# Three of eight one-hots of a group made by ScalarE, as relu(1 - (lane - place)^2), in the sums by source of a four-layer graph network

## Chip, cores and metric

The kernel runs on one core of a Trainium2 chip. The metric is the device time of one execution in microseconds (us); lower is better. The engines are TensorE (PE, with its weight loads as PEld), VectorE (DVE), ScalarE (ACT), GpSimd (POOL) and SyncE (SP).

## What is computed

Four graph layers run one after the other on 12,500 nodes with 64 features and 400,000 edges. Each starts with a layer norm and adds its result to x. The change touches the last one, whose core is

```python
i, j = edge_index            # i = src, j = dst
msg = x[j] + (edge_attr @ We + be)
agg = segment_sum(msg, i, num_segments=N)
h = (1.0 + eps) * x + agg
out = relu(h @ W1 + b1) @ W2 + b2
return (out - mu) * rsqrt(var + 1e-5) * gamma + beta
```

The segment sum goes by source, while the edges of the input lie in the order of their destination. What is summed for an edge is one row of 81 values: 64 features of the destination's x, a one, and 16 edge attributes.

## The kernel before

The kernel is a row of stages with a barrier between them. It sorts edges into slots and writes records, runs three layers that gather rows by indirect DMAs, and then, in `scatter_messages`, writes each edge's row to the DRAM array `rec2`. A row there has three bf16 parts of 81 values, which together carry the precision of f32, and one more value, the place (0 to 127) of the edge's source within its block of 128 nodes. That is 244 bf16 values, `ROW`. Padding rows have place -1. Four tiles of 128 rows (a quad) belong to one block.

The stage of the change, `source_sums`, reads `rec2` in 440 groups of 1,024 rows. A group is eight tiles (G = 8) and so two quads. All buffers form rings of eight groups (`RING2`); PSUM has a ring of four (`RING`). A loop has 55 turns and eight groups in each turn are written out (`q` = 0 to 7); the first turn is peeled. For each group

- SP issues the load of `rows[q]` (L1246), after the matmuls that read the buffer eight groups ago (`s_mm[q]`);
- ACT copies the eight places out of the rows to f32, `place[q]` (L1290), when the load has landed;
- DVE makes eight one-hots of 128x128 bf16 in `hot[q]` (L1272), by comparing the lane numbers `iotab` with a column of `place[q]`;
- PE multiplies each one-hot with the three parts of its tile, 24 matmuls of 81 columns (L1304), which leave one block sum of 128x81 for each quad;
- DVE adds the two block sums of the group before the last (`q - 2`) to `acc2` (L1265), at addresses that are read from `blks` into registers. The 16 registers of a whole turn are loaded together, in `add_group` for q = 0, so after the one-hots of q = 2.

The order on each engine is that of the code. DVE's is the one-hots of q, then the adds of q - 2. After this stage comes `last_stage`, which starts at a barrier.

Of the kernel before, what the change touches and what calls it, by code (L numbers as in the profile page):

```python
# [14 lines left out]
BF16 = mybir.dt.bfloat16  # L15
I32 = mybir.dt.int32
ALU = mybir.AluOpType
ACT = mybir.ActivationFunctionType
AX = mybir.AxisListType

P = 128
# [7 lines left out]
G = 8  # L29
# [5 lines left out]

QT = 4
RING2 = 8
QUADS = -(-((E + NB * (QT * P - 1)) // (QT * P)) // (G // QT * RING2)) * (G // QT * RING2)
GROUPS2 = QUADS * QT // G
SLOTS2 = QUADS * QT * P  # L40
EPS = 1e-5
# [12 lines left out]
ROW = PARTS * MW + 1  # L54
# [30 lines left out]
def wait_earlier(engine, semaphore, value):  # L85

    if not isinstance(value, int) or value > 0:
        engine.wait_ge(semaphore, value)
# [30 lines left out]
def build(nc, a, out):  # L119
    ctx = ExitStack()  # L120
    with ctx:
        sem = Semaphores(nc)
        rec = nc.dram_tensor("rec", (SLOTS + SPARE * G * P, RW), F32).ap()
        rec2 = nc.dram_tensor("rec2", (SLOTS2, ROW), BF16).ap()
        table = nc.dram_tensor("table", (NPAD, R * D), F32).ap()
        ptable = nc.dram_tensor("ptable", (NPAD, D), F32).ap()

        arena = ctx.enter_context(nc.sbuf_tensor("arena", [P, ARENA], F32))
        consts = Buffers(arena)
        iotaf = consts.take(P)  # L130
        ident = consts.take(P)
        iotab = consts.take(P // 2, BF16)
        identb = consts.take(P // 2, BF16)
        ones = consts.take(P)
        pidx = consts.take(1)
        epsc = consts.take(1)
        blkd = consts.take(TILES, I32)
        blks = consts.take(QUADS, I32)
        base = consts.at
        psum = ctx.enter_context(nc.psum_tensor("psum", [P, 4096], F32))  # L140

        b = Buffers(arena, base)
        ints, flts, srcl = b.take(2 * COLS, I32), b.take(2 * COLS), b.take(COLS)
        keys, off, padq = b.take(COLS, BF16), b.take(WIDE), b.take(QT * ROW // 2, BF16)
        lasts = b.take(2 * NB, I32)
        starts_stage(nc, sem, a, Buffers(arena, b.at), psum, iotaf, ident, iotab, identb, ones, pidx, epsc, blkd, blks,
                     ints, flts, srcl, keys, off, padq, lasts, rec, rec2)
        sem.end_stage()
        x = arena[:, ARENA - NB * D:ARENA]
        record_stage(nc, sem, a, b, psum, iotaf, ident, identb, epsc, ints, flts, srcl, keys, off, padq, lasts, x, rec, rec2, table)  # L150
        sem.end_stage()

        b = Buffers(arena, base)
        acc, h = b.take(NB * D), b.take(NB * D)
        shared = b.take(NB * PARTS * D // 2)
        hparts, acc2 = shared.bitcast(BF16), shared[:, 0:NB * MW]
        gather_layer(nc, sem, "g0", Buffers(arena, b.at), psum, iotaf, blkd, acc, rec, table, R_GIDX, True, False)
        sem.end_stage()
        tables_stage(nc, sem, a, "t1", Buffers(arena, b.at), psum, identb, epsc, x, acc, h, "relu", a["mh"], ptable, hparts)
        sem.end_stage()  # L160
        gather_layer(nc, sem, "g1", Buffers(arena, b.at), psum, iotaf, blkd, acc, rec, ptable, R_SRC, False, True)
        sem.end_stage()
        update_stage(nc, sem, a, Buffers(arena, b.at), psum, ident, x, acc, h)
        sem.end_stage()
        tables_stage(nc, sem, a, "t2", Buffers(arena, b.at), psum, identb, epsc, x, acc, h, None, a["w2"], table, hparts)
        sem.end_stage()
        gather_layer(nc, sem, "g2", Buffers(arena, b.at), psum, iotaf, blkd, acc, rec, table, R_GIDX, False, False)
        sem.end_stage()
        tables_stage(nc, sem, a, "t3", Buffers(arena, b.at), psum, identb, epsc, x, acc, h, "add", None, None, hparts)
        sem.end_stage()  # L170
        scatter_messages(nc, sem, Buffers(arena, b.at), psum, iotaf, identb, blkd, hparts, acc, rec, rec2)
        sem.end_stage()
        source_sums(nc, sem, Buffers(arena, b.at), psum, iotab, blks, acc2, rec2)
        sem.end_stage()
        last_stage(nc, sem, a, Buffers(arena, b.at), psum, ident, epsc, x, acc, h, acc2, out)

# [1048 lines left out]
            step(TURNS, REST)  # L1225


def source_sums(nc, sem, b, psum, iotab, blks, acc2, rec2):

    rows, hot = ([b.take(G * n // 2, BF16) for _ in range(RING2)] for n in (ROW, P))  # L1230
    place = [b.take(G) for _ in range(RING2)]
    s_ld, s_place, s_hot, s_mm = ([sem(f"c_{n}{q}") for q in range(RING2)] for n in ("ld", "place", "hot", "mm"))
    s_add = sem("c_add")
    rec2g = rec2.rearrange("(g p j) w -> g p (j w)", p=P, j=G)
    GQ = G // QT

    ps = [[psum[:, 512 * (GQ * q + u):512 * (GQ * q + u) + MW] for u in range(GQ)] for q in range(RING)]

    with nc.Block() as block:
        @block.sync  # L1240
        def _(sp):
            def step(i):
                for q in range(RING2):

                    wait_earlier(sp, s_mm[q], i)
                    sp.dma_start(rows[q], rec2g[bass.ds(i * RING2 + q, 1)].rearrange("o p w -> (o p) w")).then_inc(s_ld[q], 16)  # L1246
            peeled(sp, GROUPS2 // RING2, step)

        @block.vector
        def _(dve):  # L1250
            v = nc.vector
            regs = [dve.alloc_register(f"c_at{j}") for j in range(RING2 * GQ)]
            v.memset(acc2, 0.0).then_inc(s_add, 1)

            def add_group(i, q):

                if q == 0:
                    dve.load(regs, blks[0:1, bass.ds(i * (RING2 * GQ), RING2 * GQ)])
                ats = [dve.snap(regs[q * GQ + u], min_val=0, max_val=(NB - 1) * MW) for u in range(GQ)]
                dve.wait_ge(s_mm[q], i + 1)  # L1260
                for u in range(GQ):
                    block_sum = acc2[:, bass.ds(ats[u], MW)]

                    dve.wait_ge(s_add, i * (RING2 * GQ) + (q * GQ + u + 1))
                    v.tensor_tensor(block_sum, block_sum, ps[q % RING][u], ALU.add).then_inc(s_add, 1)  # L1265

            def step(i):
                for q in range(RING2):
                    dve.wait_ge(s_place[q], i + 1)
                    wait_earlier(dve, s_mm[q], i)  # L1270
                    for j in range(G):
                        last = v.tensor_scalar(hot[q][:, j * P:(j + 1) * P], iotab, place[q][:, j:j + 1], None, ALU.is_equal)  # L1272
                    last.then_inc(s_hot[q], 1)

                    if q >= 2:
                        add_group(i, q - 2)
                    elif not isinstance(i, int):
                        add_group(i - 1, RING2 + q - 2)
            peeled(dve, GROUPS2 // RING2, step)
            for q in (RING2 - 2, RING2 - 1):  # L1280
                add_group(GROUPS2 // RING2 - 1, q)

        @block.scalar
        def _(act):
            def step(i):
                for q in range(RING2):

                    act.wait_ge(s_ld[q], i * 16 + 16)
                    wait_earlier(act, s_hot[q], i)
                    nc.scalar.copy(place[q].rearrange("p (j o) -> p j o", o=1),  # L1290
                                   rows[q].rearrange("p (j w) -> p j w", w=ROW)[:, :, ROW - 1:ROW]).then_inc(s_place[q], 1)
            peeled(act, GROUPS2 // RING2, step)

        @block.tensor
        def _(pe):
            def step(i):
                for q in range(RING2):
                    pe.wait_ge(s_hot[q], i + 1)

                    wait_earlier(pe, s_add, i * (RING2 * GQ) + ((q - RING + 1) * GQ + 1))  # L1300
                    for j in range(G):
                        for k in range(PARTS):
                            at = j * ROW + k * MW
                            last = nc.tensor.matmul(ps[q % RING][j // QT], hot[q][:, j * P:(j + 1) * P], rows[q][:, at:at + MW],  # L1304
                                                    start=j % QT == 0 and k == 0, stop=j % QT == QT - 1 and k == PARTS - 1)
                    last.then_inc(s_mm[q], 1)
            peeled(pe, GROUPS2 // RING2, step)
# [219 lines left out]
```

## Time and profile before

| what | value |
|---|---|
| median of 3 runs | 26602.1 us (26588.82 to 26618.86) |
| profiled execution, its own time | 26631.85 us |
| its span | 26630.0 us |
| busy: PE, PEld, DVE, ACT, POOL | 9281.0, 7313.2, 10151.5, 1702.3, 15515.5 us |
| mean granted TensorE clock, 1 being 2.4 GHz | 0.523 |
| `source_sums`, first load issued to last add | about 25519 to 26522 us, 1003 us or 3.8% of the span |

Busy time is the time in which an engine has an instruction in flight. Two instructions of one engine that overlap count once, so a busy time can be smaller than the count times the mean duration. The last row is the stretch that the change can act on; the rest of the span is other stages, apart from it by barriers.

### The profile page before, as it was taken

Reading aid. Unit: us, or ns where it says so; the run is one execution under the profiler, and the core shown is the slowest. Engines: PE = TensorE matmul, PEld = TensorE weight load, DVE = VectorE, ACT = ScalarE, POOL = GpSimd, SP = SyncE. Lnnn points to the kernel's source line nnn. Section 1 sums busy time; section 2 is a strip of 40 time slices with the busy share of each in tenths; the row PEclk is TensorE's granted clock in tenths of the full one; section 3 lists DMA queues with packets and bytes.
Section 4 is the critical chain, followed back from the end, with each engine's and each line's share of the span. In section 5 each row is a group of like instructions: output and inputs, shape, how many; then the busy total and the mean of one; then the engine's idle time right before and its main releaser. Section 6 shows DMA issues by size and latency. Waiting matters only on the chain. (4 is left out here: it accounts for less than half of the span.)

```text
span 26630.0 us, 206931 instructions
## 1 busy us (share of the span) xinstructions
PE 9281.0 (35%) x47759; PEld 7313.2 (27%) x47760; DVE 10151.5 (38%) x25121; ACT 1702.3 (6%) x4834; POOL 15515.5 (58%) x16460
## 2 busy tenths in 40 slices
PE   2555555423333332222222262333333111111146
PEld 1333332223333332222222232333333111111135
DVE  6666666533333333222222242222223322222257
ACT  4000000000000000000000010000000111111101
POOL 2666666666666655555555526666665666666620
PEclk7555555555555555555555565555555555555578
DMA  3222222222222221111111132222222222222255
GB/s 96 79 79 80 79 79 69 63 52 53 53 55 53 55 47 42 50 46 46 49 47 46 47 94 52 55 53 56 53 56 46 71 72 72 71 71 71 71 164 185
DMA packets 1005338, 1785.53 MB, mean 67 GB/s; under 512 B 352516, under 2 KB 461345, under 8 KB 1004756
## 3 DMA queue, kind: packets, MB, share of 16 engines
q1 hardware_dynamic: 484516, 1127.73, 13.4%
q0 software_dynamic: 513696, 654.80, 11.4%
q10 hardware_dynamic: 7056, 2.21, 0.0%
q8 instruction: 27, 0.44, 0.0%
q14 instruction: 43, 0.35, 0.0%
HBM read 1279.39 MB, written 510.79 MB: 67 GB/s over the span
## 5 line engine op out<-in xcount | busy, mean ns | idle before, releaser
L1031 PE MATMUL psum<-arena 128*128 128x64 f32 x19392 | 4517.0, 407 | 10216.4 <-issue 6992.5
L932 POOL DMA_INDIRECT arena<-table,arena x6464 | 6115.4, 946 | 3164.5 <-issue 1938.7
L1031 PEld LDWEIGHTS psum<-arena 128*128 128x128 f32 x19392 | 4370.8, 326 | 10362.9 <-issue 8656.1
L983 DVE TENSOR_TENSOR arena<-arena,psum 128x64 f32 x9696 | 2154.3, 222 | 9784.9 <-remote 4784.5
L932 POOL DMA_INDIRECT arena<-ptable,arena x3232 | 3090.1, 956 | 2211.6 <-DMA arena<-rec 1053.4
L700 POOL DMA_INDIRECT rec<-arena x3125 | 3002.2, 961 | 2257.7 <-issue 1821.6
L1136 POOL DMA_INDIRECT rec<-arena x3232 | 3183.7, 985 | 1765.1 <-issue 954.2
L477 PE MATMUL psum<-arena 128*128 128x196 bf16 (+1 forms) x4375 | 1378.9, 429 | 2157.5 <-DVE arena L608 1297.9
L1163 DVE CAST arena<-psum 128x1536 bf16<-128x1536 f32 x404 | 710.4, 1758 | 3410.7 <-remote 3355.1
L1214 PE MATMUL psum<-arena 128*128 x3232 | 589.2, 362 | 3847.7 <-DVE arena L1163 2464.9
L1214 PEld LDWEIGHTS psum<-arena 128*128 128x128 bf16 x3232 | 352.8, 109 | 4041.1 <-issue 3953.4
L608 DVE TENSOR_TENSOR arena<-psum,arena 128x392 f32<-128x392 f32 x1875 | 923.7, 493 | 1267.0 <-remote 866.0
L477 PEld LDWEIGHTS psum<-arena 128*128 128x128 bf16 x4375 | 370.4, 115 | 3090.5 <-DVE arena L608 1624.9
L962 DVE TENSOR_TENSOR arena<-psum,arena 128x1024 f32<-128x1024 f32 x808 | 985.6, 1220 | 229.6 <-issue 223.9
L1304 PE MATMUL psum<-arena 128*128 128x81 bf16 x10560 | 607.5, 228 | 437.8 <-DVE arena L1272 431.7
L613 DVE TENSOR_REDUCE arena<-arena 128x10 f32<-128x980 f32 x625 | 734.2, 1175 | 21.6
L600 DVE TENSOR_TENSOR arena<-psum,arena 128x980 bf16<-128x980 f32 x625 | 729.9, 1168 | 0.0
L1304 PEld LDWEIGHTS psum<-arena 128*128 128x128 bf16 x10560 | 541.4, 116 | 504.0 <-issue 447.2
L1189 ACT COPY arena<-psum 128x1024 bf16<-128x1024 bf16 x404 | 408.8, 1012 | 3901.9 <-DMA rec<-arena 2743.7
L958 DVE TENSOR_TENSOR psum<-psum,arena 128x1024 f32<-128x1024 f32 x404 | 497.4, 1231 | 314.7 <-issue 313.0
L1272 DVE TENSOR_SCALAR arena<-arena 128x128 bf16<-128x128 bf16 x3520 | 610.9, 249 | 16.6 <-issue 16.6
L1377 POOL TENSOR_TENSOR arena<-arena 128x896 f32<-128x896 f32 x7 | 17.2, 2498 | 1021.5 <-DMA arena<-in_unit 1021.5
(195 smaller groups left out, 9571.1 us busy)
## 6 DMA issues: line engine op xcount, KB each, us to landing
arena<-rec SPq DMA_DIRECT2D x303, 1408.0 KB
arena<-rec SPq DMA_DIRECT2D x440, 488.0 KB
arena<-in_edge SPq DMA_DIRECT2D x625, 232.0 KB
arena<-rec SPq DMA_DIRECT2D x404, 352.0 KB
arena<-table,arena POOLq DMA_INDIRECT x6464
rec<-arena POOLq DMA_INDIRECT x6357
table<-arena SPq DMA_DIRECT2D x196, 512.0 KB
arena<-ptable,arena POOLq DMA_INDIRECT x3232
```

What stands on the lines that cost most here:

```text
L477: return nc.tensor.matmul(to, identb, one_hots, start=False, stop=False, skip_group_check=True)
L600: v.tensor_tensor(buf[g].rearrange("p (t w) -> p t w", w=NB), numsw, keyw, ALU.is_equal).then_inc(s_hot, 1)
L608: v.tensor_tensor(prod[g][:, 2 * n * WIDE:2 * n * WIDE + w], run[:, 0:w], buf[g][:, 2 * n * WIDE:2 * n * WIDE + w], ALU.mult).then_inc(s_s ...
L613: v.tensor_reduce(posf[:, g * CG * KEYS:(g + 1) * CG * KEYS], prod[g].rearrange("p (t w) -> p t w", w=NB), AX.X, ALU.add).then_inc(s_red, 1)
L700: nc.gpsimd.indirect_dma_start(rec, bass.IndirectOffsetOnAxis(ap=stage[g][:, j:j + 1], axis=0), recs[g][:, j * RW:(j + 1) * RW], None).the ...
L932: nc.gpsimd.indirect_dma_start(rows[q][:, j * D:(j + 1) * D], None, tab, bass.IndirectOffsetOnAxis(ap=idx[:, j, field:field + 1], axis=0)) ...
L962: v.tensor_tensor(ones, iotas, lanes, ALU.is_equal).then_inc(s_hot[q], 1)
L983: v.tensor_tensor(block_sum, block_sum, ps[q % SB][:, j * D:(j + 1) * D], ALU.add).then_inc(s_add[j], 1)
L1031: last = nc.tensor.matmul(ps[q % SB][:, j * D:(j + 1) * D], hot[q % SB][:, j * P:(j + 1) * P], rows[q][:, j * D:(j + 1) * D], start=True, ...
L1136: nc.gpsimd.indirect_dma_start(rec2, bass.IndirectOffsetOnAxis(ap=idx[:, j, R_SLOT:R_SLOT + 1], axis=0), rows[q][:, j * ROW:(j + 1) * ROW] ...
L1214: last = nc.tensor.matmul(ps_m[:, j * 256:j * 256 + HW], hot_t[q % 2][:, j * P:(j + 1) * P], hparts[:, bass.ds(ats[j] * PARTS, HW)], start ...
L1304: last = nc.tensor.matmul(ps[q % RING][j // QT], hot[q][:, j * P:(j + 1) * P], rows[q][:, at:at + MW], start=j % QT == 0 and k == 0, stop= ...
```

## The change

Of the eight one-hots of a group DVE makes the first five and ACT the last three (`OWN = 3`). ACT's copy of the places becomes a multiplication by -1, so `place[q]` holds minus the place. DVE's comparison is now (lane + (-place)) == 0, two operations in one instruction. ACT computes, for each of its three tiles, the square of (lane - place) into a scratch buffer `far` (a ring of two), and then with one instruction over all three tiles relu(1 - square), which is 1 where the lane is the place and 0 elsewhere. Between the multiplication and the squares, and between the squares and the relu, ACT waits on its own semaphores (`s_place[q]`, `s_far`). The relu also waits for the matmuls that read `hot[q]` a turn ago. PE waits for a new semaphore, `s_mine[q]`, ahead of the sixth tile.

```diff
+OWN = 3
-def source_sums(nc, sem, b, psum, iotab, blks, acc2, rec2):
+def source_sums(nc, sem, b, psum, iotab, ones, blks, acc2, rec2):
+    far = [b.take(OWN * P // 2, BF16) for _ in range(2)]
+    s_add, s_far = sem("c_add"), sem("c_far")
@@ vector
-                    for j in range(G):
-                        last = v.tensor_scalar(hot[q][:, j * P:(j + 1) * P], iotab, place[q][:, j:j + 1], None, ALU.is_equal)
+                    for j in range(G - OWN):
+                        last = v.tensor_scalar(hot[q][:, j * P:(j + 1) * P], iotab, place[q][:, j:j + 1], 0.0, ALU.add, ALU.is_equal)
@@ scalar
                     act.wait_ge(s_ld[q], i * 16 + 16)
                     wait_earlier(act, s_hot[q], i)
-                    nc.scalar.copy(place[q].rearrange("p (j o) -> p j o", o=1),
-                                   rows[q].rearrange("p (j w) -> p j w", w=ROW)[:, :, ROW - 1:ROW]).then_inc(s_place[q], 1)
+                    nc.scalar.mul(place[q].rearrange("p (j o) -> p j o", o=1),
+                                  rows[q].rearrange("p (j w) -> p j w", w=ROW)[:, :, ROW - 1:ROW], -1.0).then_inc(s_place[q], 1)
+                    act.wait_ge(s_place[q], i + 1)
+                    for j in range(OWN):
+                        n = G - OWN + j
+                        last = nc.scalar.activation(far[q % 2][:, j * P:(j + 1) * P], iotab, ACT.Square, bias=place[q][:, n:n + 1])
+                    last.then_inc(s_far, 1)
+
+                    act.wait_ge(s_far, i * RING2 + (q + 1))
+                    wait_earlier(act, s_mm[q], i)
+                    nc.scalar.activation(hot[q][:, (G - OWN) * P:G * P], far[q % 2], ACT.Relu, bias=ones[:, 0:1], scale=-1.0).then_inc(s_mine[q], 1)
@@ tensor
                     for j in range(G):
+                        if j == G - OWN:
+                            pe.wait_ge(s_mine[q], i + 1)
```

## Rows read from the trace of the kernel before

**Rows 1.** Groups of instructions by line, 25520 to 26530 us (busy, mean ns of one; idle before, releaser)

```profile
L1272 DVE TENSOR_SCALAR arena<-arena 128x128 bf16<-128x128 bf16 x3520 | 610.9, 249 | 16.6 <-issue 16.6
L1304 PE MATMUL psum<-arena 128*128 128x81 bf16 x10560 | 607.5, 228 | 437.8 <-DVE arena L1272 431.7 <-DVE arena L1265 3.1
L1265 DVE TENSOR_TENSOR arena<-arena,psum 128x81 f32 x880 | 208.1, 237 | 220.7 <-issue 157.4 <-DVE arena L1265 0.4
L1290 ACT CAST arena<-arena 128x8 f32<-128x8 bf16 x440 | 89.5, 203 | 947.4 <-DMA arena<-rec 947.4
```

**Rows 2.** Timeline of DVE (start, length, instructions; idle before), a turn and its end

```profile
25804.44 0.62 DVE L1265 TENSOR_TENSOR arena<-arena,psum 128x81 f32 x2 [2.87 <-issue]
...
25806.27 0.62 DVE L1265 TENSOR_TENSOR arena<-arena,psum 128x81 f32 x2
...
25814.60 1.39 DVE L1272 TENSOR_SCALAR arena<-arena 128x128 bf16<-128x128 bf16 x8 [0.31 <-issue]
...
25822.56 0.62 DVE L1265 TENSOR_TENSOR arena<-arena,psum 128x81 f32 x2 [2.90 <-issue]
```

**Rows 3.** Timeline of DVE, cut off after five one-hots

```profile
25859.30 0.90 DVE L1272 TENSOR_SCALAR arena<-arena 128x128 bf16<-128x128 bf16 x5
```

**Rows 4.** Windows, stage up to 25804.5 us, by L1290, then by L1272 (length, busy, count, PEclk, DMA share, GB/s)

```profile
25500.00:25804.50 304.50, 26.25 (x129) 0.78 0.66 213
25500.00:25804.50 304.50, 170.57 (x984) 0.78 0.66 213
```

**Rows 5.** Timeline of ACT, first casts of the stage and the 129th

```profile
25521.93 0.20 ACT L1290 CAST arena<-arena 128x8 f32<-128x8 bf16 x1 [51.67 <-DMA arena<-rec]
...
25529.76 0.20 ACT L1290 CAST arena<-arena 128x8 f32<-128x8 bf16 x1 [1.00 <-DMA arena<-rec]
...
25804.08 0.20 ACT L1290 CAST arena<-arena 128x8 f32<-128x8 bf16 x1 [2.60 <-DMA arena<-rec]
```

**Rows 6.** Timeline of PE's weight loads, at either clock

```profile
25806.48 1.63 PEld L1304 LDWEIGHTS psum<-arena 128*128 128x128 bf16 x24 [3.74 <-issue]
25816.12 0.97 PEld L1304 LDWEIGHTS psum<-arena 128*128 128x128 bf16 x24 [1.27 <-issue]
```

**Rows 7.** Windows around these loads (length, PE and PEld busy and count, PEclk, DMA share, GB/s)

```profile
25805.00:25810.00 5.00, 3.50 (x48) 3.27 (x48) 0.53 0.40 112
...
25815.00:25820.00 5.00, 2.40 (x54) 2.15 (x55) 1.00 0.88 308
```

**Rows 8.** Groups of DVE by form, whole span

```profile
L322 DVE SCALAR_TENSOR_TENSOR arena<-arena 128x3125 bf16<-128x3125 bf16 x56 | 194.8, 3478 | 28.8 <-DVE arena L322 28.4 <-DVE arena L319 0.4
L319 DVE TENSOR_SCALAR arena<-arena 128x3125 bf16<-128x3125 bf16 x2 | 2.0, 980 | 0.1
```

**Rows 9.** Groups of ACT by form, whole span

```profile
L251 ACT ACTIVATE arena<-arena 128x3125 bf16<-128x3125 bf16 x84 | 243.8, 2902 | 23.1 <-ACT arena L251 13.7 <-DVE arena L292 9.3
L1447 ACT ACTIVATE arena<-arena 128x14 f32<-128x14 f32 x7 | 2.1, 299 | 4.4 <-DVE arena L1405 4.3
L251 ACT ACT_TABLE_LOAD x1 | 1.3, 1283 | 0.6 <-PEq L1516 0.6
L580 ACT ACT_TABLE_LOAD x1 | 1.3, 1283 | 0.0
```

**Rows 10.** Timeline of ACT in the last stage, activations behind one another

```profile
26567.76 1.00 ACT L1439 ACTIVATE arena<-psum,arena 64x896 f32<-64x896 f32 x1 [0.75 <-PE psum L1463]
26568.67 0.94 ACT L1443 ACTIVATE arena<-arena 128x896 f32<-128x896 f32 x1
26569.51 0.29 ACT L1447 ACTIVATE arena<-arena 128x14 f32<-128x14 f32 x1
```

**Rows 11.** Timeline of ACT in the first stage, where it waits for itself

```profile
14.54 2.90 ACT L251 ACTIVATE arena<-arena 128x3125 bf16<-128x3125 bf16 x1 [0.18 <-ACT arena L251]
```

**Rows 12.** Timeline of ACT in scatter_messages, waits already met

```profile
24026.85 1.01 ACT L1189 COPY arena<-psum 128x1024 bf16<-128x1024 bf16 x1 [29.35 <-DMA rec<-arena]
24027.76 0.33 ACT L1183 COPY arena<-arena 128x144 bf16<-128x144 bf16 x1
```

More of the change, by code:

```diff
@@ L172, in build @@
         sem.end_stage()
-        source_sums(nc, sem, Buffers(arena, b.at), psum, iotab, blks, acc2, rec2)
+        source_sums(nc, sem, Buffers(arena, b.at), psum, iotab, ones, blks, acc2, rec2)
         sem.end_stage()
@@ L1225, in _ @@
             step(TURNS, REST)
-def source_sums(nc, sem, b, psum, iotab, blks, acc2, rec2):
+def source_sums(nc, sem, b, psum, iotab, ones, blks, acc2, rec2):
     rows, hot = ([b.take(G * n // 2, BF16) for _ in range(RING2)] for n in (ROW, P))
     place = [b.take(G) for _ in range(RING2)]
-    s_ld, s_place, s_hot, s_mm = ([sem(f"c_{n}{q}") for q in range(RING2)] for n in ("ld", "place", "hot", "mm"))
-    s_add = sem("c_add")
+    far = [b.take(OWN * P // 2, BF16) for _ in range(2)]
+    s_ld, s_place, s_hot, s_mine, s_mm = ([sem(f"c_{n}{q}") for q in range(RING2)] for n in ("ld", "place", "hot", "mine", "mm"))
+    s_add, s_far = sem("c_add"), sem("c_far")
     rec2g = rec2.rearrange("(g p j) w -> g p (j w)", p=P, j=G)
```

## The prediction

> **What bounds the kernel now.** Only one stage changes, so I read that stage and little else. The groups by line for its stretch come first [rows 1]. PE is idle 438 us there and waits nearly always for the one-hots of L1272. ACT is idle 947 us and waits only for loads. DVE waits for nobody: the idle time before its one-hots is 16.6 us, that before its adds 157.4 us, and both are "issue", so DVE's own sequencer and not another engine. DVE is therefore the bound, and the reader should check this on its timeline [rows 2]. A step (eight one-hots, two adds) takes 25806.27 - 25804.44 = 1.83 us, and once in a turn 2.87 us pass before an add, where the 16 registers are loaded, and 0.31 us at the loop's end. A turn takes 25822.56 - 25804.44 = 18.12 us: about 8 x 1.83, 2.87, 0.31 and a rest of 0.3. Fifty-five turns are 997 us, which is the stage.
>
> Next, how far the loads are ahead. Before 25804.5 us ACT had begun 129 casts and DVE 984 one-hots, or 123 groups [rows 4]. So the cast at 25804.08 [rows 5] is that of the 129th group, the first of a turn. The adds at 25804.44 are the first of their turn and stand behind its third one-hots; five more steps follow, and the next turn's first one-hots, those of the 129th group, start at 25814.60, behind the loop's 0.31 us [rows 2]. A load has landed 10.5 us before DVE wants it. The buffer came free when the group eight before it was multiplied, one turn less about 3 us after its one-hots began (1.39 for them, up to 1.63 for PE at the lower clock [rows 6, 7]), so near 25799.5, and the load took some 4.6 us. At the stage's start loads landed about every 1.2 us [rows 5]. They are no limit until a group takes near that.
>
> **What the change takes off DVE.** Eight one-hots take 1.39 us [rows 2], five take 0.90 us [rows 3], so 0.49 us a group or 3.9 us a turn goes. DVE alone would need 18.1 - 3.9 = 14.2 us a turn. The comparison gets a second operation. No row has exactly this form with a pointer. A two-operation TENSOR_SCALAR in bf16 with immediates takes 980 ns for 3125 elements [rows 8], 0.31 ns an element with its fixed part in, so the second operation does not stop the fast rate there, and I cost it at nothing. Bound from above: at the pace that L322 shows (3478 ns for 3125, 1.1 ns each) each of five would take some 128 x 0.8 = 0.10 us longer, 4.1 us a turn, and DVE would be back at 18.3 us.
>
> **What it puts on ACT.** ACT did 0.20 us a group. Now it does five instructions in a chain.
> - The multiplication, 128x8: as the cast, 0.203 us [rows 1].
> - A square, 128x128 with a pointer bias. Between L1447 (14 elements, 299 ns) and L251 (3125 elements, 2902 ns), both with a pointer bias, the slope is 0.837 ns and the fixed part 0.287 us [rows 9]. That gives 0.394 us for 128 elements.
> - The relu, 128x384 with a pointer bias: 0.287 + 0.32 = 0.607 us.
> - Instructions behind one another overlap. L1439 starts at 67.76 and takes 1.00, L1443 starts 0.91 later; L1443 takes 0.94 and L1447, with a pointer, starts 0.84 later [rows 10]. So each costs its duration less 0.095 us if the next need not wait: a square 0.30, the relu 0.51.
> - The two waits for itself. The nearest row is ACT's loop in the first stage, 0.18 us idle before an instruction that waits for the one ahead, 13.7 us over 83 waits, or 0.165 on the mean [rows 9, 11], with a loop's branch in it. On DVE two adds with such a wait between them take 0.62 where each takes 0.237 [rows 1, 2], a gap of 0.145. I take 0.165. Below, nothing is excluded but the overlap that is lost.
> - Waits that are already met cost nothing: L1183 starts 0.91 after L1189 (1.01 long), although a wait stands between them in the code [rows 12]. So the wait for the load, for `s_hot` and for `s_mm`, all of events some groups old, are free.
>
> Sum: 0.203 + 0.165 + 2 x 0.30 + 0.394 + 0.165 + 0.51 = 2.04 us a group. With the loop's end as DVE shows it, 0.31 us, a turn is 8 x 2.04 + 0.31 = 16.6 us. This is above DVE's 14.2, so ACT is the new bound and DVE, with 2.4 us left over in a turn, absorbs most of its 2.87 us of register loading as a short lag behind ACT. ACT is not held by that lag, as it waits only for events of the turn before.
>
> **What else hangs on it.** PE's 24 weight loads of a group take 1.63 us where the granted clock is 0.53, the 1.2 GHz level, and 0.97 us where it is 1.00, at 2.4 GHz [rows 6, 7], below 2.04 at either. It does five tiles while ACT is at its three and then waits for ACT, which adds three tiles (0.6 us at most) behind the relu. A load has a turn of 16.6, less ACT's 2.04, the last three tiles and DVE's lag of up to about 3 us: some 11 us for a landing time of 4.6. So the loads stay hidden, and ACT never waits. In the first groups ACT has a start: its first load lands at 25521.93 [rows 5], before DVE has cleared `acc2`.
>
> From there 440 x 2.04 + 55 x 0.31 = 915 us lead to 26436.6 and, with PE and two adds, to 26438; the stage's last add now ends near 26521.6. By turns it is the same: (18.12 - 16.63) x 55 = 82 us. The profiled execution has 26631.85 us, 0.1% above the median of the runs; 82 us off it are 26550, or 0.31%, and the median becomes 26520 us.
>
> **A rule that speaks against it.** ACT pays for its three one-hots 3 x 0.30 + 0.10 + 0.33 + 0.51 = 1.84 us where DVE paid 0.49 [rows 2, 3, 9]. The Trainium skill, "ScalarE: Activation LUTs", section "Rules for kernel authors", says that relu and products belong on VectorE, up to about three times faster in bf16; here the trace makes it near four. By the rule the change adds 1.35 x 440 = 594 us of engine time. That would be lost only if ACT were already full, and ACT was idle 947 of 1003 us [rows 1]; what decides is only whether the chain on ACT stays under 18.12 / 8 = 2.26 us.
>
> **The rivals.**
> 1. *DVE stays the bound.* If squares overlap more than other pairs and the waits cost little, ACT's group falls under 14.2 / 8 = 1.77 us; then the turn is 14.2 and 215 us go: 26387 us. Needed are 0.27 us less than the rows give, and the pairs in [rows 10] speak against it.
> 2. *The gain is eaten.* With no overlap between the pointer activations (3 x 0.095 more) ACT's group is 2.33 us and the turn 18.9: +45 us. Or the two-operation comparison runs slowly, DVE at 18.3 us: +10 us. Anything between 2.10 and 2.34 us a group lies within 0.2%, which is what a measurement of this kernel can tell from no change (53 us). About 26600 us.
> 3. *Slower: ACT's waits for itself are long.* The place is the two waits in each group. The dearest such wait in the trace is DVE's in its loop at L322, 28.4 us over 55, or 0.52 us [rows 8]. At that price the group is 2.04 + 2 x 0.35 = 2.75 us, the turn 22.3 and the kernel 231 us slower, 26833 us. It decides from 0.32 us a wait (2.35 us a group). Against it stands ACT's own 0.165.
> 4. *Table loads.* Should Square, Relu and the multiplication lie in different tables, each group would load twice at 1.283 us [rows 9], the group is 4.6 us and the kernel near 1,000 us slower. It decides from about three loads a turn. Against it: the trace has two loads in all, at L251 and L580, and the last stage runs Relu, Square and Sqrt in turn behind them without one. The Trainium skill, "ScalarE: Activation LUTs", section "What ACT_TABLE_LOAD costs", counts 2.66 us for a switch where the row shows 1.283 for the load itself; by it this case would be some 7.4 us a group and over 2,200 us slower.
>
> **How the numbers follow.** The forecast (group of 1.85 to 2.10 us) gets 0.62, rival 1 with everything under 1.85 us 0.06, rival 2 0.21, rival 3 0.09, rival 4 0.02. The first two are faster by over 0.2%: 0.68. Rival 2 is 0.21, the last two 0.11. The likeliest time is 26520 us. 1.85 us a group is a turn of 15.1, 165 us less. The range runs from 26450, a little under 1.87 us, to 26605, which takes in the better part of rival 2; outside it lie about 0.05 below and 0.15 above.
>
> **What would show it.** In the profile after: L1272 x2200 with a mean near 249 ns; DVE waiting for ACT before its one-hots for some 130 us in all; the register load still 2.87 us. ACT's timeline packed, with no idle time on DMA beyond a few us, and gaps only ahead of the first square and the relu, 0.165 us each; squares near 0.39, the relu near 0.61 us, busy about 750 us in the stage (1.71 a group). PE's wait moves from L1272 to ACT. No table load in the stage. It goes wrong if a turn on ACT is not near 16.6 us: by the gaps, by the overlap of the squares, or because ACT still waits for loads, which would mean that the loads land later than 4.6 us.

## The result and the profile after

The changed kernel takes 26414.44 us (median of 4 runs, 26406.61 to 26444.47) against 26610.31 us of the kernel before (4 runs): a ratio of 0.993, 95% interval 0.9912 to 0.9947. It is 196 us faster. The forecast was 26520 us with a range of 26450 to 26605, so the direction was right and the time lies 36 us below the range. It is 27 us above rival 1's 26387 us, in which DVE stays the bound.

The first view is the groups of instructions by line, 25520 to 26340 us, columns as in [rows 1].

```profile
L1317 PE MATMUL psum<-arena 128*128 128x81 bf16 x10560 | 547.5, 223 | 303.6 <-DVE arena L1274 300.3 <-DVE arena L1267 2.5
L1297 ACT ACTIVATE arena<-arena 128x128 bf16<-128x128 bf16 x1320 | 433.6, 391 | 14.3
L1274 DVE TENSOR_SCALAR arena<-arena 128x128 bf16<-128x128 bf16 x2200 | 395.5, 249 | 17.1 <-issue 17.1
L1302 ACT ACTIVATE arena<-arena 128x384 bf16<-128x384 bf16 x440 | 270.6, 615 | 14.3
L1267 DVE TENSOR_TENSOR arena<-arena,psum 128x81 f32 x880 | 207.7, 236 | 243.3 <-issue 178.4 <-DVE arena L1267 0.4
L1292 ACT ACTIVATE arena<-arena 128x8 f32<-128x8 bf16 x440 | 88.5, 201 | 66.3 <-DMA arena<-rec 65.3
```

DVE still waits for nobody: its idle time is "issue", as before [rows 1]. The forecast had it waiting some 130 us for ACT. The new instructions have the forecast durations (squares 391 ns, relu 615, multiplication 201, the two-operation comparison 249). What differs is what lies between them. This is the timeline of ACT over one group:

```profile
25900.96 0.20 ACT L1292 ACTIVATE arena<-arena 128x8 f32<-128x8 bf16 x1
25901.19 0.98 ACT L1297 ACTIVATE arena<-arena 128x128 bf16<-128x128 bf16 x3
25902.21 0.61 ACT L1302 ACTIVATE arena<-arena 128x384 bf16<-128x384 bf16 x1
25902.73 0.20 ACT L1292 ACTIVATE arena<-arena 128x8 f32<-128x8 bf16 x1
```

From 25901.16 to 25901.19 and from 25902.17 to 25902.21 ACT waits for itself. Over the stage, the idle time before the squares and before the relu is 14.3 us each, or 0.03 us a wait in 440 groups, where the forecast had 0.165. The group takes 25902.73 - 25900.96 = 1.77 us. The next view is DVE's timeline, a turn's end to end, to be read beside [rows 2].

```profile
25900.98 0.62 DVE L1267 TENSOR_TENSOR arena<-arena,psum 128x81 f32 x2 [3.28 <-issue]
...
25908.64 0.90 DVE L1274 TENSOR_SCALAR arena<-arena 128x128 bf16<-128x128 bf16 x5 [0.32 <-issue]
...
25911.33 0.90 DVE L1274 TENSOR_SCALAR arena<-arena 128x128 bf16<-128x128 bf16 x5
25915.49 0.62 DVE L1267 TENSOR_TENSOR arena<-arena,psum 128x81 f32 x2 [3.27 <-issue]
```

This turn is 25915.49 - 25900.98 = 14.51 us. The stall at the register load has grown from 2.87 to 3.27 us. The register load has a row of its own, on DVE's sequencer; the first row is of the kernel before, the second of the changed one (minimum, median and maximum in ns):

```profile
L1258 DVEq TENSOR_LOAD <-arena x55: 3602/3614/3641, 25529.0 to 26506.2; - x55
```

```profile
L1260 DVEq TENSOR_LOAD <-arena x55: 3604/3618/3649, 25532.8 to 26319.9; - x55
```

From the first one-hot of the stage to its last add it is 26521.4 - 25527.1 = 994.3 us before and 26332.6 - 25532.3 = 800.3 after, 18.08 and 14.55 us a turn. That is 194 us; the profiled executions differ by 187.4 us, and the remaining +6.7 us lie before the stage (5.2) and behind it (1.5).

### The profile page after: what moved, and what is told of

The parts are those of the page before. It is cut to its first block and busy times, and to the rows that moved or that the text cites. A ratio compares the mean times of both kernels' runs of the same rounds, so it can differ in the third digit from the quotient of the medians.

```text
span 26442.7 us, 208289 instructions
## 1 busy us (share of the span) xinstructions
PE 9223.4 (35%) x47759; PEld 7289.5 (28%) x47760; DVE 9926.7 (38%) x23801; ACT 2369.0 (9%) x6594; POOL 15473.5 (59%) x16460
## 5 line engine op out<-in xcount | busy, mean ns | idle before, releaser
L1015 ACT ACTIVATE arena<-arena 128x512 f32<-128x512 f32 x404 | 254.6, 630 | 5054.0 <-issue 2706.7
L1317 PE MATMUL psum<-arena 128*128 128x81 bf16 x10560 | 547.5, 223 | 303.6 <-DVE arena L1274 300.3
```

## The experiments

The runs that follow were made in three batches, between which the stages ahead of `source_sums` changed their time: the kernel before had medians of 26774.6 us (e1 to e4), 22730.7 (e5 to e8) and 22675.0 (e9 to e11), and the changed kernel began the stage at 25532.3 us in its first profile and at 21596.8 in that of e9. Why is open; the first two batches are on record with the same chip. In the stage itself the changed kernel took 800.3 and 800.0 us. So each median is given as its difference to the kernel before in its own batch. These differences agree with those of the stage within 18 us; where the two differ, the stage is the better measure of what the edit did. The stage is from the first one-hot to the last add, from the start times in each trace, and a turn is a 55th of it.

| kernel | difference to before, us | ratio (95%) | stage, us | turn, us |
|---|---|---|---|---|
| before | 0 | | 994.3 | 18.08 |
| changed | -195.9 | 0.993 (0.9912 to 0.9947) | 800.3 | 14.55 |
| changed, again (e9) | -189.7 | 0.9916 (0.9898 to 0.9934) | 800.0 | 14.55 |
| two on ACT (e1) | -121.1 | 0.9955 (0.9938 to 0.9971) | 862.2 | 15.68 |
| four on ACT (e2) | -36.8 | 0.9987 (0.9977 to 0.9996) | 950.4 | 17.28 |
| form alone (e3) | +1.4 | 1.0002 (0.9993 to 1.0012) | 994.3 | 18.08 |
| ACT left out (e4) | -175.7 | 0.9932 (0.9915 to 0.9948) | 800.7 | 14.56 |
| two more waits (e5) | -96.3 | 0.9958 (0.9941 to 0.9974) | 899.6 | 16.36 |
| registers by group, three on ACT (e6) | -215.3 | 0.9906 (0.989 to 0.9923) | 777.6 | 14.14 |
| registers by group, two on ACT (e7) | -250.0 | 0.989 (0.9873 to 0.9906) | 746.6 | 13.57 |
| registers by group, none on ACT (e8) | -164.9 | 0.993 (0.9913 to 0.9946) | 832.4 | 15.13 |
| four registers at a time, two on ACT (e10) | -167.5 | 0.9925 (0.9908 to 0.9943) | 820.5 | 14.92 |

### Which engine sets the turn: two or four one-hots on ACT

```diff
-OWN = 3
+OWN = 2
```

> ACT makes two one-hots of a group and DVE six. Theory A: the changed kernel is bound by DVE, whose turn is about 14.55 us, and ACT's group of 1.77 us (14.2 us a turn) lies just under it. Then one more one-hot on DVE adds 0.163 x 8, less the part that hides under the register load, about 1.2 us a turn, and the time is 26414 + 66 = 26480 us; ACT's group falls to about 1.36 us and ACT waits for loads. Theory B: ACT, with its loads, sets the turn of the changed kernel. Then ACT's shorter group makes the kernel faster than 26414 us or leaves it there.

Measured: 75 us slower than the changed kernel by the differences, 61.9 us by the stage (66 expected). ACT's group became shorter and the kernel longer, so Theory B falls. Waiting time moved to ACT, which waits 279.5 us for loads:

```profile
L1267 DVE TENSOR_TENSOR arena<-arena,psum 128x81 f32 x880 | 208.1, 236 | 234.9 <-issue 171.6 <-DVE arena L1267 0.4
L1292 ACT ACTIVATE arena<-arena 128x8 f32<-128x8 bf16 x440 | 91.2, 207 | 281.6 <-DMA arena<-rec 279.5
```

```diff
-OWN = 3
+OWN = 4
```

> ACT makes four one-hots of a group, DVE four. ACT must become the bound, so its chain is read at its full price. Theory A (a wait of ACT for its own instruction leaves a gap of 0.03 us): group 0.23 + 3 x 0.298 + 0.425 + 0.62 = 2.17 us, turn 17.4 us, 154 us more than the changed kernel: 26568 us. Theory B (such a wait costs the 0.165 us of the prediction, and the changed kernel escapes it in some way): group 2.44 us, turn 19.5 us, 26687 us, slower than the kernel before.

Measured: 36.8 us below the kernel before (42 expected). A group of DVE and a stretch of ACT's timeline:

```profile
L1274 DVE TENSOR_SCALAR arena<-arena 128x128 bf16<-128x128 bf16 x1760 | 325.7, 250 | 218.2 <-ACT arena L1292 218.2
```

```profile
26103.77 0.20 ACT L1292 ACTIVATE arena<-arena 128x8 f32<-128x8 bf16 x1
26104.00 1.28 ACT L1297 ACTIVATE arena<-arena 128x128 bf16<-128x128 bf16 x4
26105.31 0.72 ACT L1302 ACTIVATE arena<-arena 128x512 bf16<-128x512 bf16 x1
26105.94 0.20 ACT L1292 ACTIVATE arena<-arena 128x8 f32<-128x8 bf16 x1
```

A group takes 26105.94 - 26103.77 = 2.17 us, as computed with 0.03 us for a wait. Here DVE waits for ACT ahead of its one-hots, 218.2 us, the sign of an ACT bound that the changed kernel does not have. With three on ACT the bound is DVE, with four it is ACT, and the crossing lies between.

### The new form alone

```diff
-  v.tensor_scalar(hot..., iotab, place..., None, ALU.is_equal)
+  v.tensor_scalar(hot..., iotab, place..., 0.0, ALU.add, ALU.is_equal)
-  nc.scalar.copy(place..., rows...)
+  nc.scalar.mul(place..., rows..., -1.0)
```

> The kernel before with the multiplication by -1 on ACT and the two-operation comparison on DVE for all eight one-hots; nothing moves to ACT. Theory A: the new form costs nothing, DVE's instruction stays at 249 ns and its turn at 18.1 us: 26610 us within 0.1%. Theory B: the second operation slows an instruction by up to 0.10 us: up to 6.4 us a turn, 350 us slower.

Measured: +1.4 us, the stage the same to 0.1 us, 249 ns for a comparison of either form. The step of the prediction that costed it at nothing holds.

### ACT left out

```diff
-                    act.wait_ge(s_place[q], i + 1)
...
-                        if j == G - OWN:
-                            pe.wait_ge(s_mine[q], i + 1)
+            for q in range(RING2):
+                v.memset(hot[q][:, (G - OWN) * P:G * P], 0.0).then_inc(s_far, 1)
```

The squares, the relu and their waits are left out with this, and PE waits once, at the start, for the zeroing. Three of eight tiles are then not summed.

> The changed kernel without ACT's squares, relu and their waits: the last three one-hot tiles of each ring buffer are zeroed once at the start, so three of eight tiles are not summed; DVE, PE, the adds and the loads do the same work as in the changed kernel. Theory A (DVE is the bound and ACT is hidden): 26414 us within 0.1%, plus some 3 us for the zeroing. Theory B (ACT holds the turn in part): faster than the changed kernel by what ACT costs, 20 us or more.

Measured: the stage is 800.7 us, that of the changed kernel 800.3. The median difference, -175.7, is 14 to 20 us short of the changed kernel's, within the 0.1% of Theory A but no proof of it by itself. The stage, which is what the theories speak of, is equal, so the 14 to 20 us lie outside it: in the four profiles of this batch the first one-hot starts anywhere from 25664.1 to 25700.2 us. ACT's squares and relu cost the changed kernel nothing in the stage.

### The price of a wait of ACT for itself

```diff
-                        last = nc.scalar.activation(far..., iotab, ACT.Square, bias=place...)
-                    last.then_inc(s_far, 1)
-                    act.wait_ge(s_far, i * RING2 + (q + 1))
+                        nc.scalar.activation(far..., iotab, ACT.Square, bias=place...).then_inc(s_far, 1)
+                        act.wait_ge(s_far, i * (RING2 * OWN) + (q * OWN + j + 1))
```

> The changed kernel, with ACT waiting for its own last instruction after each of the three squares and not only after the third: two more waits a group. Theory A (a wait of ACT for itself leaves 0.03 us and costs the overlap of 0.095, 0.125 in all): ACT's group is 1.77 + 0.25 = 2.02 us, the turn 16.2 us, 88 us above the changed kernel and 108 below the one before. Theory B (0.165 us a gap, as the prediction had it): group 2.29 us, turn 18.3 us, 10 us above the one before.

Measured: 93 us above the changed kernel of e9 by the differences to before, 99.6 by the stage (88 expected). ACT's timeline:

```profile
21860.10 0.20 ACT L1292 ACTIVATE arena<-arena 128x8 f32<-128x8 bf16 x1
21860.33 1.27 ACT L1297 ACTIVATE arena<-arena 128x128 bf16<-128x128 bf16 x3
21861.63 0.61 ACT L1300 ACTIVATE arena<-arena 128x384 bf16<-128x384 bf16 x1
21862.15 0.20 ACT L1292 ACTIVATE arena<-arena 128x8 f32<-128x8 bf16 x1
```

Three squares of 401 ns take 1.27 us, so (1.27 - 0.40) / 2 = 0.435 us from start to start: 0.034 us of gap. Without the wait it is (0.985 - 0.391) / 2 = 0.297 us. A wait between two instructions costs 0.14 us, most of it the overlap that is lost. The group is 2.05 us. This also shows how narrow the case is: a group of 2.05 us, nearly that of the forecast, gives -96 us, the forecast's -82.

The row from which the forecast took 0.165 us is the loop of the first stage. In the changed kernel it was written out in part:

```diff
-            with act.Fori(2 * SD + 1, NB) as i:
-                act.wait_ge(s_sign, i - 2 * SD)
-                source_signs(i)
+            for n in range(2 * SD + 1, 2 * SD + 22):
+                act.wait_ge(s_sign, n - 2 * SD)
+                source_signs(n)
+            with act.Fori((2 * SD + 22) // 2, NB // 2) as i:
+                for k in range(2):
+                    act.wait_ge(s_sign, i * 2 + (k - 2 * SD))
+                    source_signs(i * 2 + k)
```

> The changed kernel, with ACT's loop of the first stage, from which the prediction took 0.165 us for a wait of ACT for itself, partly written out: 21 passes with constant waits, then a loop with two passes in a turn. Theory A (0.165 us was the loop's branch and its register instructions, which start only after the wait): the passes written out have a gap of 0.03 to 0.05 us between the accumulator read and the next activation, those in the middle of the loop's body little more, those at its turn still about 0.17. Theory B (the gap belongs to the wait behind an accumulator read): 0.165 us in all three.

The timeline of ACT at the seam: the first three rows are passes written out, the rest passes of the loop, two to a turn. The kernel ran once, in 22476.4 us, and only its timeline is used.

```profile
74.91 0.19 ACT L252 ACTIVATION_READ_ACCUMULATOR arena<-arena 128x1 f32 x1
75.13 2.90 ACT L252 ACTIVATE arena<-arena 128x3125 bf16<-128x3125 bf16 x1
77.94 0.18 ACT L252 ACTIVATION_READ_ACCUMULATOR arena<-arena 128x1 f32 x1
78.30 2.90 ACT L252 ACTIVATE arena<-arena 128x3125 bf16<-128x3125 bf16 x1 [0.18 <-ACT arena L252]
...
84.62 2.90 ACT L252 ACTIVATE arena<-arena 128x3125 bf16<-128x3125 bf16 x1 [0.16 <-ACT arena L252]
...
87.78 2.90 ACT L252 ACTIVATE arena<-arena 128x3125 bf16<-128x3125 bf16 x1 [0.16 <-ACT arena L252]
```

And that line's register instructions (duration in ns, first and last start):

```profile
L252 ACTq FUSED_REGOPS  x62: 74/74/94, 78.2 to 270.4; - x62
```

Written out, the gap is 75.13 - 75.10 = 0.03 us, behind the same accumulator read, so Theory B falls. Theory A is right that it is not the wait, and wrong about the branch: in the loop every gap is 0.16 to 0.18 us, in the middle of a turn and at its end alike. What all 62 passes of the loop have, and none of those written out, is a register instruction of 74 ns (94 at most) on the activation's line. The activation's bias and its accumulator's column are chosen by the loop variable, so their addresses are worked out between the wait and the activation. In `source_sums` the addresses of ACT's operands are constants.

The start times in the traces divide the gap. At 84.28 us the accumulator read starts and takes 0.187; the register instruction starts 0.030 us behind its end, takes 0.074, and the activation starts 0.054 us behind that: 0.158 in all. Where the register instruction takes longer, the gap is longer by as much: 0.164 us with 80 ns, which is 81 of the 83 passes of the changed kernel, and 0.183 with 94 ns, the first pass of this loop. A rival is that a wait is dear when its value comes from a register, as it does in this loop. Against it stand the 54 turns of `source_sums`: their waits take their values from the loop variable too, and leave 0.03 us. No run took the register instruction out and left the rest of the loop as it was.

### The registers

The register load was the largest stall of DVE in both kernels. Each group's two addresses were loaded with its adds, in three kernels that differ in the number of ACT's one-hots (e6 to e8). A fourth (e10, two one-hots on ACT) loads four addresses ahead of every second group's adds. The edit of e6:

```diff
-                if q == 0:
-                    dve.load(regs, blks[0:1, bass.ds(i * (RING2 * GQ), RING2 * GQ)])
-                ats = [dve.snap(regs[q * GQ + u], ...) for u in range(GQ)]
+                dve.load(regs, blks[0:1, bass.ds(i * (RING2 * GQ) + q * GQ, GQ)])
+                ats = [dve.snap(regs[u], ...) for u in range(GQ)]
```

> The changed kernel, but DVE loads the two block addresses of a group just ahead of its adds, and not 16 once in a turn. The 16 take 3.62 us of DVE's sequencer, eight on PE 2.06, two on ACT 0.64; so about 0.2 us and 0.21 a register. Theory A: the load, 0.62 us, lies mostly beside the queued one-hots, DVE's turn falls below 14 us and ACT's 14.2 us is the bound: 10 to 30 us below the changed kernel (ACT then sets the turn, DVE waits for it before its one-hots). Theory B: a load holds the sequencer so that one-hots are not queued beside it; then each of eight steps grows by 0.6 us, less than the 3.3 us saved by little: 14.5 to 16 us a turn, up to 80 us slower.

> As the last, with two one-hots of a group on ACT and six on DVE. Theory A: a step of DVE is 0.90 + 0.16 + 0.45 + at most 0.2 us, so 1.5 to 1.7 and a turn of 12.4 to 14 us; ACT needs 11: 30 to 120 us below the changed kernel. Theory B: slower than the changed kernel.

> The kernel before (eight one-hots on DVE) with the two addresses loaded for each group. Theory A: the register load hides under 1.39 us of one-hots, the turn falls from 18.1 to about 15.1 us: 165 us below the kernel before, most of what the change gave. Theory B: the loads show in full, eight of 0.62 us for one of 3.6: 60 us slower.

Theory A held in all three. With three on ACT the turn is 14.14 us, ACT's eight groups of 1.77, and DVE waits for ACT (first row, e6). With two on ACT it is 13.57 us and DVE waits for nobody (second, e7):

```profile
L1273 DVE TENSOR_SCALAR arena<-arena 128x128 bf16<-128x128 bf16 x2200 | 397.7, 250 | 58.0 <-ACT arena L1291 53.5 <-issue 0.4
```

```profile
L1273 DVE TENSOR_SCALAR arena<-arena 128x128 bf16<-128x128 bf16 x2640 | 467.5, 250 | 16.3 <-issue 16.3
```

With none on ACT the kernel before becomes 164.9 us faster without the change.

> The changed kernel as it is, as a control beside the two that follow: 196 us below the kernel before, its stage 800 us from the first one-hot to the last add.

> Two one-hots of a group on ACT, and DVE loads four addresses for two groups at a time. Loading two took 0.536 us, 16 took 3.62, so 0.10 us and 0.22 a register, and four take about 1.0. With two by two DVE's turn was 13.56 us. Theory A (the load hides when it is shorter than the one-hots in the queue, 1.06 us): as that kernel or up to 10 us faster. Theory B (what doesn't fit beside the one-hots shows): every second step is about 0.4 us longer, a turn of 14 to 15 us, 20 to 60 us slower than two by two.

The control gave 800.0 us for the stage. Four at a time gave 820.5, 74 us more than two by two: Theory B, whose turn of 14 to 15 us held (14.92) and whose 20 to 60 us was too little. Every second step shows a stall. The loads of four (e10) and of two (e7):

```profile
L1260 DVEq TENSOR_LOAD <-arena x220: 958/965/994, 21591.2 to 22407.8; - x110
```

```profile
L1259 DVEq TENSOR_LOAD <-arena x440: 517/536/559, 21624.6 to 22369.0; - x147
```

A load takes 0.536 us for 2 registers, 0.965 for 4 and 3.61 for 16, near 0.10 us and 0.22 a register. What is seen of it follows from when it starts. From the start of its step's first one-hot the load of 16 begins after 0.33 us where the step has eight one-hots (before), after 0.26 with six (e1) and after 0.22 with five (changed). That is 0.05 us and 0.034 for each one-hot, so by these times the load begins when the sequencer has handed the one-hots over, and not when DVE, at 0.163 us apiece, has done them. The adds start 0.32 us behind the load's end. So from the first one-hot to the adds it is 4.26 us with eight one-hots, 4.20 with six and 4.16 with five (medians over the turns; with four, where DVE waits for ACT ahead of them, 4.07). Taking three one-hots away in that step shortens it by 0.10 us and not by 0.49.

With short loads the same sum holds as long as it is above the one-hots' own time. Six one-hots take 0.98 us to the adds without a load (e1, and e10's steps that have none), 1.10 with a load of two (e7) and 1.54 with a load of four (e10). For a load of four the sum is 0.05 + 6 x 0.034 + 0.965 + 0.32 = 1.54. Eight one-hots take 1.30 us without a load (before) and with a load of two (e8) alike: there the load is hidden wholly.

## Why the prediction was wrong

That the kernel gets faster was forecast rightly, but with ACT as the bound, and the chance given to the bound that held was 0.06.

**The step that failed** is in "What it puts on ACT": "The two waits for itself. ... I take 0.165." It measured 0.03 us, 0.27 us less a group for the two. The row was that of a wait with a register instruction behind it. The prediction noted the loop's branch in that gap, and took the number as if the wait were all of it. ACT's turn came out at 16.6 us where it is 14.2, so ACT became the bound in the forecast and is none in the kernel. With it falls the bound that it set for rival 1 ("Needed are 0.27 us less than the rows give"): precisely these 0.27 us were there.

**A smaller term of the same sum**, the loop's end at 0.31 us a turn on ACT, measured nothing that can be seen: where ACT is the bound, the turn is just its eight groups, 8 x 1.77 = 14.16 us for 14.14 in e6 and 8 x 2.17 = 17.36 for 17.28 in e2 (where DVE's later start counts in). DVE's 0.32 us at its own loop's end is there.

**The rest of ACT's sum was right:** 0.20 for the multiplication, 0.298 a square, 0.39 for the last, 0.52 for the relu until the next may start. With 0.03 twice it is 1.77 us, a turn of 14.2 us.

**DVE's turn** was put at 14.2 and measured 14.55 us. It had the register load's stall at 2.87 us as before; the stall is what is left of the load after the one-hots, and with fewer one-hots more is left, 3.24 us on the mean. Seven steps of a turn became 0.49 us shorter and the one with the load 0.10: 3.53 us, which is 18.08 - 14.55, where the forecast had 3.9. That is the missing 0.37 us a turn, or 20 us in all. It made the miss smaller: ACT's sum was 2.4 us a turn too long, DVE's 0.37 too short. Without this growth the kernel would have been near rival 1's 26387 us; ACT, at 14.2, would have allowed it.

**Loads.** ACT waited for loads 31 times, 65.3 us of which 51.7 are the stage's start, so 14 us, while it was ahead of DVE. At 25804.5 us ACT had begun 154 groups and DVE 755 one-hots, 151 groups. The loads stay hidden, but ACT's lead is three groups now and not nearly six [rows 4].

**The form, PE, the tables.** The form cost nothing (e3). PE's wait stayed on L1274, 300.3 us, and did not move to ACT, since ACT is no bound. There is no table load in the stage. A slip of the range changes nothing: 26450 us belong to 1.88 us a group by the prediction's own sum, not to a little under 1.87. Rivals 3 and 4 need waits ten times dearer than the trace shows and table loads that do not occur. The rule of the Trainium skill that was weighed, that relu and products belong on VectorE ("ScalarE: Activation LUTs", "Rules for kernel authors"), did not decide, as argued; e2 is where it begins to: the fourth one-hot moved to ACT costs 159 us against the changed kernel (150 by the stage).

**What is shown and what is argued.** Shown: DVE bounds the changed kernel (e1, e4), a wait of ACT for itself leaves 0.03 us (the timeline, e2, e5), 0.165 us was not the wait (e11), and what the register load adds (e6 to e10). Read from start times and not from a run of its own: that the address instruction is the cause of the gap in the first stage.

## What to carry to other kernels

A gap read from a loop has the register instructions in it that lie between the wait and the instruction, so before it is carried to another place look whether the operands there are addressed by a register too. When two engines end up within a few per cent of one another, give both sums the same care: here the forecast was wrong by 0.27 us in 2 and by 0.37 in 14, and the first of them chose the rival. And a stall that is called "issue" should be looked up on its sequencer before work is moved off the engine: loading two addresses at a time was worth 165 us of the kernel before, and together with two one-hots on ACT 250 us (ratio 0.989, 0.9873 to 0.9906), more than that alone or than the change alone.

## What the runs showed of the hardware

In two of the four kernels without DVE's long register stall TensorE kept its upper clock. The windows of the kernel with registers by group and two one-hots on ACT (e7), of the one with none on ACT (e8) and of the changed kernel (e9), all in the stage's middle (columns as in [rows 6, 7], with DVE, ACT and POOL behind PE and PEld):

```profile
21700.00:22300.00 600.00, 388.56 (x8495) 341.41 (x8493) 520.02 (x2831) 494.50 (x1416) 0.00 (x0) 1.00 0.86 295
21700.00:22300.00 600.00, 372.52 (x7613) 328.58 (x7610) 542.39 (x3176) 64.79 (x319) 0.00 (x0) 0.95 0.83 265
21700.00:22300.00 600.00, 407.76 (x7894) 382.06 (x7890) 402.45 (x2296) 565.82 (x1646) 0.00 (x0) 0.84 0.79 275
```

Weight loads of e7, at a turn's end and behind it, and of the changed kernel, behind its gap and later in the same turn:

```profile
21921.57 0.96 PEld L1316 LDWEIGHTS psum<-arena 128*128 128x128 bf16 x24 [1.08 <-issue]
21923.28 0.97 PEld L1316 LDWEIGHTS psum<-arena 128*128 128x128 bf16 x24 [0.75 <-issue]
```

```profile
25800.55 5.04 PEld L1317 LDWEIGHTS psum<-arena 128*128 128x128 bf16 x96 [3.73 <-DVE arena L1267]
25805.93 0.97 PEld L1317 LDWEIGHTS psum<-arena 128*128 128x128 bf16 x24 [0.34 <-issue]
```

The granted clock is 1.00, so 2.4 GHz throughout, in e7, whose weight loads pause some 0.7 us between groups and 1.1 at a turn's end, and in e6, where the longest pause is 0.9 us. It is 0.84 on the mean in the changed kernel, whose weight loads stop for 3.73 us once in a turn and whose next groups take 1.26 us each where later ones take 0.97. That the long stall is gone is not enough: in e8, with pauses of 0.87 us between groups and 1.27 at a turn's end, the mean is 0.95, and stretches at 1.2 GHz return about once in a turn; in e10, with pauses up to 1.2 us, it is 0.94. DVE's waits for PE come to at most 0.8 us in any of these kernels, so the clock explains none of their times.
